# Decay attention on 128-token chunks with compact 32-token blocks, one layer norm for two, and a new issue order in delta attention

## The reference, cut to what matters

```python
# delta attention, per head: short convolution of 4 taps, then SiLU
y = sum(xp[:, i:i + t, :] * w[:, i] for i in range(4)); y = silu(y)
# state S of 128 x 128 per head; three (k, v, beta) per token
S = S * exp(g_t)
for i in range(3):
    S = S + beta_i * k_i outer (v_i - k_i @ S)
o_t = q_t @ S

# decay attention, on the layer norm xn of the normed stream; 2 heads of 64 channels
xn = layernorm(layernorm(x)) * ln_g + ln_b
w = sigmoid(xn @ Wx @ Ww + bw); k = xn @ Wk; v = xn @ Wv; r = sigmoid(xn @ Wr)
state = (1 - w_t) * state + k_t outer v_t
out_t = r_t @ state
y = out @ Wo
```

## Time and profile before

| | |
|---|---|
| median of three runs | 3561.93 us (3559.84 to 3565.68) |
| the profiled execution | 3555.57 us, span of its instructions 3553.5 us |
| TensorE busy | 3264.9 us (92%) |
| VectorE busy | 2732.4 us (77%) |
| ScalarE busy | 2264.8 us (64%) |
| GpSimd busy | 2070.6 us (58%) |
| granted TensorE clock, mean | 0.936 |

### The profile page before, as it was taken

The page is one execution under the profiler, slowest core; times in us unless marked ns, Lnnn a source line. Parts: engine busy times, 40 slices in busy tenths (PEclk is TensorE's granted clock), DMA queues, the critical chain, the costliest instruction groups (busy, mean ns, idle before and its releaser), DMA issues. The chain is left out here.

```text
span 3553.5 us, 83210 instructions
## 1 busy us (share of the span) xinstructions
PE 3264.9 (92%) x26980; PEld 2519.4 (71%) x26980; DVE 2732.4 (77%) x5990; ACT 2264.8 (64%) x6803; POOL 2070.6 (58%) x3164
## 2 busy tenths in 40 slices
PE   5359999999999999999999999999899977598998
PEld 3247888888888888888888888887644446576444
DVE  3468999999999999999999999986444448944443
ACT  3368888888888888888888888884433330002333
POOL 1278888888888888888888888885100005700000
PEclk8679999999999999999999999999999987566999
DMA  2647787777777787777777788774233200001333
GB/s 54 174 127 174 173 178 178 175 168 178 182 177 174 171 188 175 171 176 186 175 176 174 181 176 176 168 177 107 67 134 128 95 10 1 1 1 25 135 133 113
DMA packets 612599, 491.41 MB, mean 138 GB/s; under 512 B 498396, under 2 KB 525564, under 8 KB 606028
## 3 DMA queue, kind: packets, MB, share of 16 engines
q1 hardware_dynamic: 609868, 479.80, 55.6%
q10 hardware_dynamic: 2304, 6.29, 0.6%
HBM read 285.69 MB, written 200.25 MB: 137 GB/s over the span
## 5 line engine op out<-in xcount | busy, mean ns | idle before, releaser
L732 POOL TENSOR_TENSOR X<-X,tmp 96x31 f32<-96x31 f32 (+15 forms) x992 | 535.2, 540 | 77.8
L729 POOL TENSOR_TENSOR tmp<-At,X 96x31 f32<-96x31 f32 (+15 forms) x992 | 482.8, 487 | 122.8 <-DMA At<-n_d 67.5
L1654 POOL TENSOR_TENSOR b_P<-b_P,b_tmp 128x512 f32<-128x512 f32 x80 | 114.5, 1431 | 439.2 <-DVE b_tmp L1672 434.5
L1090 PE MATMUL PP<-xn,wk 128*128 128x268 f32 x1024 | 311.6, 407 | 59.9 <-DMA tk<-in_conv_q_dram 40.5
L697 POOL TENSOR_TENSOR Sg<-S,gend 128x512 f32<-128x512 f32 x256 | 276.6, 1080 | 108.6 <-DVE S L916 108.6
L792 ACT ACTIVATE conv_k<-PP,tk 128x256 f32<-128x256 f32 x512 | 236.4, 472 | 105.5 <-PE PP L1090 99.8
L756 ACT ACTIVATE recA<-TG 128x128 f32<-128x128 f32 x1024 | 266.6, 276 | 31.5 <-PE TG L1141 31.5
L764 ACT ACTIVATE recA<-TG,es 96x128 f32<-96x128 f32 x1024 | 274.6, 370 | 17.3 <-DVE es L940 17.2
L1054 PEld LDWEIGHTS RB<-rhs,Yf 96*96 96x96 f32 x2048 | 239.5, 162 | 64.8 <-DVE rhs L905 52.5
L1054 PE MATMUL RB<-rhs,Yf 96*96 96x128 f32 x2048 | 276.2, 278 | 9.8 <-DVE rhs L905 9.3
L1044 PE MATMUL RA<-S,kqgB 128*96 128x128 f32 x2048 | 275.1, 277 | 0.7 <-DVE S L916 0.7
(11 more groups left out here) (293 smaller groups left out, 8223.3 us busy)
## 6 DMA issues: line engine op xcount, KB each, us to landing
kqg_d<-kqgA SPq DMA_DIRECT2D x128, 512.0 KB, 5.1
kqgB<-kqg_d SPq DMA_DIRECT2D x128, 512.0 KB, 7.3
rec_d<-recA SPq DMA_DIRECT2D x128, 480.0 KB, 3.7
recB<-rec_d SPq DMA_DIRECT2D x128, 480.0 KB, 8.6
f1gates<-f1gates_d SPq DMA_DIRECT2D x24, 1024.0 KB, 6.6
f2gates<-f2gates_d SPq DMA_DIRECT2D x24, 1024.0 KB, 6.8
gdec<-gdec_d SPq DMA_DIRECT2D x128, 128.0 KB, 6.6
apk_d<-apkA SPq DMA_DIRECT2D x128, 128.0 KB, 2.5
```

What stands on the lines that cost most here:

```text
L729: nc.gpsimd.tensor_tensor(t, At[q % 2][:, j, j + 1:].unsqueeze(2).broadcast_to(sh), X[q % 2][:, j, 0:cols].unsqueeze(1).broadcast_to(sh), ...
L732: nc.gpsimd.tensor_tensor(x, x, t, ALU.subtract).then_inc(sub_ev, 1)
L1090: mm(out, w, x, start=True, stop=True).then_inc(tile_mm[i], 1)
```

## The change

Delta attention computes the same with the same instructions in another order. VectorE's `taps_` becomes `tap1`, `tap2`, `tap3`, with other work between some of them, and `sc` becomes `ss_`, `rinv_`, `step_`. The orders of all five queues are new.

Decay attention changes in structure:

- The two norms become one: with v the variance of the stream, both together divide by the root of (1 + eps)·v + eps², which ScalarE takes with `scale` and `bias`. Gain, bias and all weights are loaded by SyncE during it. The projections, the levels and the walk are one block.
- Levels 0 to 5 (`near`) multiply only the diagonal 32 x 32 blocks, 64 small matmuls per level and sequence, into a compact `Pc` of 128 x 512 per sequence: one masked operation in place of four, a predicated copy instead of product and addition. GpSimd only clears P.
- Two more levels (`far`) have rectangles with no mask: 32 x 32 matmuls at level 6, 64 x 64 at level 7, copied into P by ScalarE. ScalarE also spreads Pc into P (`spread`).
- The first two levels of a sequence are issued between the projections of later tiles.
- F comes straight from ScalarE as sigmoid of the negative; the third VectorE operation of a tile goes.
- The walk has 8 chunks of 128 tokens. P·V and state·rF accumulate in one PSUM bank, so the addition L1774 goes.

```diff
@@ delta attention: SyncE, GpSimd, ScalarE, VectorE, TensorE @@
                 dec_load(f)
+                kqg_store(f - 1)
+                rec_store(f - 1)
                 ap_store(f - 1)
                 y_load(c + 1)
-                rec_store(f - 1)
-                kqg_store(f - 1)
...
+                x_zero(*group_at(f, 3))
                 fo_(r - 1)
                 kqg(f - 1)
                 sg(r, 0)
-                subst(*group_at(f, GROUP + 1), range(0, 3))
+                rk_(f - 1)
+                subst(*group_at(f, GROUP + 1), range(0, 6))
                 sg(r, 1)
-                rk_(f - 1)
-                subst(*group_at(f, GROUP + 1), range(3, 6))
-                x_zero(*group_at(f, 3))
                 subst(*group_at(f, GROUP + 1), range(6, 12))
...
-                qsilu(f - 1)
+                xt(*group_at(f, 2 * GROUP + 1))
                 tap0(c, "v0")
-                mo_(r - 1, 1)
+                tap0(c, "v1")
                 ksum_(f - 1, 1)
-                tap0(c, "v1")
+                ksum_(f - 1, 0)
+                wev(r, 0)
                 tap0(c, "v2")
-                xt(*group_at(f, 2 * GROUP + 1))
-                wev(r, 0)
-                ksum_(f - 1, 0)
                 gate_(c)
                 zev(c)
+                tap0(f, "k1")
+                mo_(r, 0)
                 tap0(f, "k0")
-                tap0(f, "k1")
-                kr(f - 1, 1)
                 kr(f - 1, 0)
                 vsilu(c)
-                q2_(f - 1)
+                kr(f - 1, 1)
                 tap0(f, "k2")
                 w12(c)
                 wev(r, 1)
+                q2_(f - 1)
                 tap0(f, "q")
-                mo_(r, 0)
+                mo_(r, 1)
+                yev(c)
                 ksilu(f)
-                yev(c)
+                qsilu(f)
...
-                sup(r - 1, 1)
-                taps_(c, "v0")
+                tap1(c, "v0")
+                osb_(r - 1)
+                tap2(c, "v0")
                 rhs_(r, 0)
-                osb_(r - 1)
-                taps_(c, "v1")
+                tap3(c, "v0")
+                tap1(c, "v1")
                 og_(r - 1)
-                taps_(c, "v2")
+                tap2(c, "v1")
+                tap3(c, "v1")
+                ss_(f - 1)
+                rinv_(f - 1)
                 acc_(r - 1)
-                sc(f - 1)
+                tap1(c, "v2")
+                step_(f - 1)
+                tap2(c, "v2")
+                tap3(c, "v2")
                 sup(r, 0)
                 es_(f - 1)
-                taps_(f, "k0")
-                taps_(f, "k1")
+                tap1(f, "k1")
+                tap1(f, "k0")
+                tap2(f, "k0")
+                tap3(f, "k0")
                 rhs_(r, 1)
+                tap2(f, "k1")
+                ap(f - 1, 0)
+                tap3(f, "k1")
+                tap1(f, "k2")
+                tap2(f, "k2")
                 ap(f - 1, 1)
-                ap(f - 1, 0)
-                taps_(f, "k2")
-                taps_(f, "q")
+                tap3(f, "k2")
+                tap1(f, "q")
+                tap2(f, "q")
+                tap3(f, "q")
                 vr(c, 1)
+                sup(r, 1)
                 vr(c, 0)
...
                 v_tile(c, 0)
-                o_(r - 1, 1)
+                v_tile(c, 1)
                 ktr(f - 1, 1)
-                v_tile(c, 1)
                 ks(r, 0)
                 ktr(f - 1, 0)
+                zm(c)
+                ot(r - 1)
+                w_(r, 0)
                 v_tile(c, 2)
-                w_(r, 0)
-                ot(r - 1)
-                zm(c)
+                out(r - 1)
                 gate_tile(c)
-                out(r - 1)
                 sr(r, 0)
+                k_tile(f, 1)
+                o_(r, 0)
                 k_tile(f, 0)
-                k_tile(f, 1)
                 wm(c)
-                o_(r, 0)
                 ks(r, 1)
-                gram(f - 1, 1)
                 gram(f - 1, 0)
                 k_tile(f, 2)
                 w_(r, 1)
+                gram(f - 1, 1)
                 k_tile(f, 3)
-                vtr(c, 0)
+                o_(r, 1)
                 m3(c)
                 vtr(c, 1)
+                vtr(c, 0)
                 sr(r, 1)
@@ decay attention @@
+        def steps():
+            for i in range(NT):
+                yield "tile", i
+                for l in range(2):
+                    b, odd = divmod(i - 2 - l, 2)
+                    if not odd and 0 <= b < B - 1:
+                        yield "near", (l, b)
+            yield "near", (0, B - 1)
+            yield "near", (1, B - 1)
+            for l in range(2, LV + 1):
+                for b in range(B):
+                    yield ("near" if l < MASKED else "far"), (l, b)
...
+            def near(l, b):          # TensorE
...
+                for q in range(NGB):
+                    for h in range(2):
+                        for c in range(4):
+                            t0 = (b * NGB + q) * 128 + 32 * c
+                            o = pair[pair_of(n)][32 * c:32 * c + 32, h, 32 * q:32 * q + 32]
+                            last = mm(o, kB[64 * h:64 * h + 64, t0:t0 + 32], rF[64 * h:64 * h + 64, t0:t0 + 32], start=True, stop=True)
...
+            def near(l, b):          # VectorE
...
+                if l == 0:
+                    nc.vector.tensor_tensor(dst, src, mask, ALU.mult).then_inc(p_ev, 1)
+                else:
+                    dve.wait_ge(p_ev, near_no[l - 1, b] + 1)
+                    nc.vector.copy_predicated(dst, mask.bitcast(mybir.dt.uint32), src).then_inc(p_ev, 1)
...
+            for b in range(B):       # ScalarE, after its eight tiles
+                far(MASKED, b)
+            for b in range(B):
+                spread(b)
+            for b in range(B):
+                far(LV, b)
...
+            for n in range(NGB):     # TensorE, the walk
+                need(pe, o_ev, n - 2)
+                if n + 1 < NGB - 1:
+                    update(n + 1)
...
+                        mm(o[64 * h:64 * h + 64, b * 128:(b + 1) * 128], V[:, i, 64 * h:64 * h + 64], P[:, i, h, :], start=b == 0, stop=False)
+                need(pe, s_ev, n - 1)
+                for b in range(B):
+                    last = mm(o[:, b * 128:(b + 1) * 128], S[:, n % 2, b, :], rF[:, b * T + 128 * n:b * T + 128 * n + 128], start=False, stop=b == B - 1)
```

More of the change, by code:

```diff
@@ L173, in layernorm, with _ @@
         block = ctx.enter_context(nc.Block())
+        if fetch is not None:
+            @block.sync
+            def _(sp):
+                fetch(sp)
         @block.tensor
@@ L941, in es_, with tap_of @@
                                         step_s[:, :].unsqueeze(2).broadcast_to([R, U, TC]), ALU.mult).then_inc(es_ev, 1)
[L943 to L945 removed]
+            def tap_of(N, name, j):
                 i, x = TILES[name], N // KSTEPS % 2
@@ new lines, in decay_attention @@
+        kt_mm, kt_ev, u_mm, u_ev, s_ev, a_mm, o_ev, y_mm, y_ev, z_ev = (
+            sem(n) for n in ("kt_mm", "kt_ready", "u_mm", "u_ready", "s_ready", "a_mm", "o_ready", "y_mm", "y_ready", "s_zero"))
+        NEAR = MASKED * B
+        FAR = [(l, b) for l in range(MASKED, LV + 1) for b in range(B)]
+        NP = NEAR + len(FAR)
+        pair_of = lambda n: 2 + n % 2 if n < 2 * B else n % 4
+        before = {n: max((m for m in range(n) if pair_of(m) == pair_of(n)), default=None) for n in range(NP)}
@@ new lines, in _, with tile, far, spread @@
+        @block.scalar
+        def _(act):
+            def tile(i):
+                act.wait_ge(zx, i + 1)
+                need(act, z_mm, i - 2)
+                nc.scalar.activation(z1[:, i % 2, :], bank[0], ACT.Copy).then_inc(zx_ev, 1)
+                act.wait_ge(r_mm, i + 1)
+                nc.scalar.activation(rF[:, TILE * i:TILE * (i + 1)], bank[2], ACT.Sigmoid).then_inc(r_ev, 1)
+                act.wait_ge(z_mm, i + 1)
+                nc.scalar.activation(F[:, TILE * i:TILE * (i + 1)], bank[0], ACT.Sigmoid, scale=-1.0, bias=neg_bw[:, :]).then_inc(f_ev, 1)
+            def far(l, b):
+                n = far_no[l, b]
+                H = 1 << (l - 1)
+                act.wait_ge(p_mm, n + 1)
+                for c in range(0, 128, 2 * H):
+                    src = pair[pair_of(n)][c:c + H, :, 0:H * NGB].rearrange("p h (q t) -> p h q t", t=H)
+                    dst = P[c:c + H, b * NGB:(b + 1) * NGB, :, c + H:c + 2 * H].rearrange("p q h t -> p h q t")
+                    last = nc.scalar.activation(dst, src, ACT.Copy)
+                last.then_inc(far_ev, 1)
+            def spread(b):
+                act.wait_ge(p_ev, near_no[MASKED - 1, b] + 1)
+                G = slice(b * NGB, (b + 1) * NGB)
+                for c in range(4):
+                    o = slice(32 * c, 32 * c + 32)
+                    nc.scalar.activation(P[o, G, :, o], Pc[o, G, :, :], ACT.Copy).then_inc(spread_ev, 1)
+            act.wait_ge(nb_ev, 1)
+            for i in range(NT):
```

(15 more changed lines are left out.)

457 lines of the change are left out of this document (221 added, 236 removed).

## The result

The changed kernel takes 3325.05 us (median of 4 runs, 3322.43 to 3328.68), the kernel before 3561.83 beside it: ratio 0.9337, 95% interval 0.9322 to 0.9352. The forecast was 3349 with a range of 3310 to 3425. The profiled execution took 3328.68 us, 226.9 less than that of before. Of these, 16.2 lie ahead of the first mixture (its first instruction comes at 2544.12 instead of 2560.33), 208.7 in the decay attention with its norm (196.7 us from mixture to mixture, for 405.4), and 2 elsewhere.

What follows compares the result with a forecast made beforehand. TensorE, at 17.68 us per iteration, was to become delta attention's only bound; VectorE bounds the old decay levels, TensorE the walk. Delta -5 and decay -208 us total -213: 3561.93 - 213 = 3349 us, range 3310 to 3425.

Steps and rivals of the forecast that it cites:

- The decay attention, -208 forecast: Decay attention and its norms: steps sum to 197 us for 405.4, so 208 us less.
- Delta attention, -5 forecast: Delta attention loop: steady part gains nothing, first eleven iterations 0.5 us each; -5 us, bounds -28 to +30.
- as many: TensorE in delta attention: changes of tile shape, some 0.1 us each, stay equal in number, so it stays at 17.68 us.
- VectorE 0.96 us less: Delta attention: 8 dependent pairs of 16 remain on VectorE, saving 8 x 0.12 = 0.96 us per iteration, to about 16.5.
- the margin at `gate_tile`: Delta attention: `og_`, `out` and `acc_` follow `ot` closely, with about 0.3 us to spare at `gate_tile`.
- Norm, 25 forecast: Decay attention's norms: one of two goes; of 52.0 us some 25 stay, weights and gain load beneath it.
- Projections and six steps, 52 forecast: Decay projections stay at 38 us; six `near` between them cost TensorE 14 us, at 2.4 us per 64 small matmuls.
- 18 steps, 52 forecast: The other 18 `near` follow at VectorE's pace, 18 x 2.65 = 48 us, plus about 4 waiting for a merge.
- The rival with slow small matmuls: Levels: small matmuls at m3's pace, 5.0 us per 64, TensorE bounds; 58 us more, 3407 us; chance 0.13.
- Rectangles, spread, transposes, 24 forecast: After the last near merge: far merges and ScalarE's copies some 17 us, transposes and their copies 7; 24 us.
- Walk, 44 forecast: Eight walk steps between 31 us at full clock and 62 at 1.2 GHz; taken as 40, plus 4 for end and barriers.
- The merges, 0.62 from start to start: Levels: with GpSimd idle, each of VectorE's three merges falls from 1.6 us to 0.7, start to start 0.62.

Runs made afterwards that it cites:

- spacers: Changed kernel with five one-column operations more on VectorE per iteration, behind the third taps of v0, v1, v2, k0 and k2, nothing reordered: 3337.01 us (0.9363).
- taps-together run: Changed kernel with the taps of a tile one behind the other again on VectorE, 13 dependent neighbours in place of 8: 3459.74 us (0.973).
- the additions: Changed kernel with GpSimd adding one scratch tile to another, 36 times 128x512, while the levels run: 3333.69 us, one execution.
- levels early: Changed kernel with ScalarE's spreads ahead of its level-6 copies and ten instead of six level steps between the projection tiles: 3325.46 us (0.9343).

## Why the prediction was right, and where its steps were not

The total was right within 24 us; several of its terms were off and partly cancelled. The decay attention, -208 forecast and -208.7 measured, agrees so closely by luck: 12.75 us too much for the walk and 7.2 for the projections stood against 13.6 too little for the level steps and 5.6 for the rectangles and transposes. Of the 24 us, 11 are delta attention's, 1 the decay attention's and 2 elsewhere; the other 10 are the distance of the two profiled executions from their medians, 6.4 us below for before and 3.6 above for the changed kernel.

- *Delta attention, -5 forecast, -16 measured.* The mechanism held: TensorE has no wait for `rhs` in three iterations of four, small gaps show on VectorE, the wait for `At` fell to one of 1.3 us in the window of the earlier trace rows, the fourth iteration is longer. Two sizes were off. TensorE's floor is 17.52 us, not 17.68. I had counted changes of tile shape as equal ("as many") since the number of places stayed, but `o_` and `m3` beside each other have almost the same shape and cost 0.13 us less than `o_` beside a tile. And `xt` costs 0.79 us, not 1.0: ScalarE had 1.17 us idle ahead of its first `w` copy. Four iterations are 70.9 us for 71.6. The steady part, for which I had forecast nothing, gave most of it. All 128 `ss_`, before and after:

```profile
L926 DVE TENSOR_SCALAR ss<-ksum x128: 159/183/1181, 152.5 to 2379.2; 128x8 f32<-128x8 f32 x128
...
L933 DVE TENSOR_SCALAR ss<-ksum x128: 159/161/1665, 154.6 to 2357.6; 128x8 f32<-128x8 f32 x128
```

The first comes 2.1 us later than before. The eleven iterations behind it gain 3.5 us (forecast 5), the other 116 gain 20.2 (forecast 0), and from the last `ss_` to the mixture it takes 186.5 us for 181.2, 5.3 more.
- *"VectorE 0.96 us less" as the reason.* The spacers show that about 0.3 us more on VectorE costs 0.04. So shorter work on VectorE is not what the order buys. In the kernel before no weight load waited for a tap between 506 and 2296 us; what fell against it is the wait for `rhs`, from 30.6 us in 100 iterations to 11.2 in 26 of 101, and TensorE's own 0.16 us. The taps-together run shows what such an order must keep, last taps that end before the tile that needs their bank: there that costs 1.06 us. I had followed the margin at `gate_tile` (0.3 us), and it was indeed a thin one; the other thin one was at k2.
- *Norm, 25 forecast, 25.5.* Right.
- *Projections and six steps, 52 forecast, 44.8.* The small matmuls are cheaper than I took them: 64 in 1.58 us at a granted clock of about 0.5, 0.025 us each, for 0.037 from the earlier trace rows. Those rows hold a pause. The same 4.7 us of the kernel before as a timeline, at a granted clock of 0.50 too:

```profile
55.51 2.45 PE L313 MATMUL ga<-wba,xn 128*32 128x32 f32 x162 [6.33 <-DMA after_bd<-in_c_after_bd_dram]
58.97 1.50 PE L313 MATMUL ga<-wba,xn 128*32 128x32 f32 x94 [1.02 <-issue]
```

Without the 1.02 us on "issue" it is 0.029 us each. A pause of the kind that decided the level steps could be seen here before the change. The Trainium skill, TensorEngine Tiling (Array Packing), section Instruction Overhead, with its 60 cycles per matmul would give 3.2 us per 64 even at full clock, by my estimate from it; the trace has 1.58 us, half of that, at the lower clock, so here the measurement decides.
- *18 steps, 52 forecast, 65.6.* This is the step of the prediction that failed: "the other 18 follow at VectorE's pace". VectorE's cost was right (2.53 us measured where it bounds, 2.65 forecast) and so was that TensorE's burst is shorter. What I left out, and put at nothing without a reason, is a third bound, the supply of TensorE's instructions: 256 of them per step, a transfer of 16 KB, every 3.3 to 3.9 us. The rival with slow small matmuls had the right place, not the mechanism. The Trainium skill, Runtime: NRT & Kernel Launch, section Instruction fetch mechanics, says that an engine's instructions come in blocks of 16 KiB, 256 instructions, and that crossing a block is mostly hidden. The size agrees with the transfers here. "Hidden" does not, where a block is used up in 1.6 us.
- *Rectangles, spread, transposes, 24 forecast, 29.6.* ScalarE's 18.48 us in a row came as I had summed them; that it starts only when TensorE's late matmuls are there adds the rest.
- *Walk, 44 forecast, 31.25.* I had taken a value between the two clocks. It ran at 1.00 throughout, at my floor: 3.9 us per step forecast there, 31.25 / 8 = 3.9 measured, the end included. That the larger operands brought the clock is not shown; no run changes the walk alone.
- *The merges, 0.62 from start to start.* Right, and shown to be GpSimd's doing. The Trainium skill, GPSIMD Engine Reference, section Specifications, names contention between GpSimd and VectorE instructions with two SBUF inputs. The trace agrees: beside the additions, those with two took 1.0 to 1.4 us in the mean, the one with PSUM did not change.

## What to carry to other kernels

Packing many tiny matmuls trades columns for instructions, and instructions have a rate of their own: when a stretch shows TensorE idle on "issue" with no engine full, count the instruction transfers in the DMA view against its steps before moving other work about, and look whether a pause falls where the program has no wait. An engine's slack counts only where it lies; check an order by who frees the buffer that the bound engine takes next. And to learn whether an order or a sum binds, add small operations without moving anything.

## What the runs showed of the hardware

- TensorE's instructions came at 256 per 3.3 to 3.9 us in the level steps (18 transfers of 16 KB in 65.6 us). In the 12 us of the DMA view, a transfer started about 0.6 us before a burst ended, and the next burst 2.3 to 2.9 us after the transfer. When VectorE slowed its steps to 5.0 us, the bursts kept 3.63 us until TensorE waited for VectorE. Behind a projection tile 193 matmul records with their weight loads ran without a pause (levels early, 1.89 us from 2885.25), so the supply gets ahead where TensorE's instructions are longer.
- 64 matmuls of 32 columns over four column groups took 1.58 us at a granted clock of about 0.5, and 1.29 us between the projection tiles, where the clock was 0.96 in the mean.
- VectorE products with two SBUF operands took 0.68 us alone and 1.14, 1.64 and 1.75 us beside a GpSimd addition; a predicated copy from PSUM took 0.72 in both cases.
